# Two conditioned sequence layers: key exponentials of layer 0 scaled on POOL and turned by DVE blocks and a scratch in batches 1 to 6

## The reference, cut to what matters

```python
xn = _ln(x, ln_w, ln_b)
q = xn @ Wq + bq
k = xn @ Wk + bk + (1.0 - src_mask) * -1000000.0
q = softmax(q.reshape(b, t, h, dh), axis=-1)
k = softmax(k.reshape(b, t, h, dh), axis=1)          # over the tokens
v = ((xn @ Wv + bv) * src_mask).reshape(b, t, h, dh)
att = einsum('bnhd,bnhl->bhdl', k, v)
y = einsum('bnhd,bhdl->bnhl', q, att).reshape(b, t, d)
hh = _ln(y, ln2_w, ln2_b) * (1.0 + scale) + shift    # scale, shift from silu(emb) @ W_emb
return x + silu(hh) @ W_out + b_out
```

## Time and profile before

| | |
|---|---|
| median of three runs | 1324.58 us (1324.13 to 1326.19) |
| profiled execution | 1324.74 us |
| its span, first to last instruction | 1322.9 us |
| mean granted TensorE clock | 0.969 |
| PE busy | 1265.4 us, 96% |
| PE's weight loads busy | 1010.9 us, 76% |
| DVE busy | 1012.7 us, 77% |
| ACT busy | 902.6 us, 68% |
| POOL busy | 499.3 us, 38% |
| layer 0 | to about 470 us, layer 1 behind it |

### The profile page before, as it was taken

How to read it: one execution, slowest core, us unless ns; L and a number is a source line. 1 busy time by engine, 2 the same in 40 slices (tenths; PEclk the granted TensorE clock), 3 DMA queues, 4 the chain that set the end, 5 groups by cost and what they waited for, 6 DMA issues and landing times.

```text
span 1322.9 us, 24811 instructions
## 1 busy us (share of the span) xinstructions
PE 1265.4 (96%) x9256; PEld 1010.9 (76%) x9256; DVE 1012.7 (77%) x2027; ACT 902.6 (68%) x2051; POOL 499.3 (38%) x451
## 2 busy tenths in 40 slices
PE   8998999999999799899999999999999999999998
PEld 6786888888888687577787788788788788788666
DVE  6678898898988856766876876876876876877766
ACT  5232433424326438788898898898898898898984
POOL 0526548366383730102612612612612512522502
PEclk9998999999999899899999999999999899999989
DMA  9245374664646455855455465464465464454422
GB/s 334 76 152 156 101 222 121 206 194 120 214 127 215 144 197 174 241 164 162 149 172 158 152 174 156 152 175 149 158 174 150 150 182 144 153 172 144 136 75 81
DMA packets 123081, 214.13 MB, mean 162 GB/s; under 512 B 8704, under 2 KB 38456, under 8 KB 122064
## 3 DMA queue, kind: packets, MB, share of 16 engines
q1 hardware_dynamic: 122960, 212.55, 52.1%
HBM read 130.14 MB, written 81.85 MB: 160 GB/s over the span
## 4 chain that ended last, share of the span: by engine, by line
PE 64%; DVE 13%; ACT 11%; POOL 7%; issue 4%; DMA 1%; SPq 0%; DVEq 0%; POOLq 0%; ACTq 0%
PE ps L612 13%; PE ps L613 12%; PE ps L614 12%; PE ps L794 8%; PE ps L768 6%; PE ps L776 6%; ACT ps L958 5%; PE ps L607 3%; DVE st L1080 2%; ACT Pb L968 2%; PE ps L719 2%; POOL yb L1388 2%; DVE xr L1098 2%; POOL yb L1444 1%; POOL vt L1395 1%
## 5 line engine op out<-in xcount | busy, mean ns | idle before, releaser
L958 ACT ACTIVATE ps<-ps,cT 128x512 f32<-128x512 f32 x512 | 346.8, 717 | 19.6 <-DVE cT L1243 19.2
L1243 DVE TENSOR_REDUCE cT<-ps 128x1 f32<-128x512 f32 x512 | 320.6, 682 | 43.8 <-PE ps L768 42.2
L968 ACT ACTIVATE Pb<-ps 128x512 f32<-128x512 f32 x512 | 268.5, 661 | 46.0 <-PE ps L776 43.8
L768 PE MATMUL ps<-Ks,Qs 98*128 98x512 f32 x512 | 185.0, 423 | 16.7 <-ACT ps L958 16.5
L776 PE MATMUL ps<-Qs,Ks 100*128 100x512 f32 x512 | 159.1, 408 | 1.1 <-ACT ps L958 0.5
L768 PEld LDWEIGHTS ps<-Ks,Qs 98*128 98x128 f32 x512 | 96.6, 192 | 67.2 <-ACT ps L958 41.8
L958 ACT ACTIVATION_READ_ACCUMULATOR ps<-ps,cT 128x1 f32 x512 | 134.8, 263 | 0.0
L776 PEld LDWEIGHTS ps<-Qs,Ks 100*128 100x128 f32 x512 | 95.8, 189 | 37.8 <-ACT Pb L968 12.8
L612 PE MATMUL ps<-xTh,Wh_k 128*128 128x512 f32 x256 | 105.6, 413 | 14.0 <-DVE xTl L1102 11.0
L612 PE MATMUL ps<-Wh_o,sTh 128*128 128x512 f32 x256 | 104.7, 409 | 5.1 <-DVE sTl L1220 4.5
L1379 POOL TENSOR_SCALAR vf<-vf,mk 128x512 f32<-128x512 f32 x16 | 25.0, 1564 | 209.7 <-DVE vf L1153 209.7
(11 more groups left out here) (178 smaller groups left out, 2826.3 us busy)
## 6 DMA issues: line engine op xcount, KB each, us to landing
Qs<-stack_scratch SPq DMA_DIRECT2D x32, 768.0 KB
Ks<-stack_scratch SPq DMA_DIRECT2D x32, 768.0 KB
stack_scratch<-sg_q SPq DMA_DIRECT2D x32, 512.0 KB, 2.7
stack_scratch<-sg_k SPq DMA_DIRECT2D x32, 512.0 KB, 2.6
wr<-in_x SPq DMA_DIRECT2D x32, 256.0 KB, 5.0
x_scratch<-wr SPq DMA_DIRECT2D x32, 256.0 KB, 2.4
stack_scratch<-sg_q SPq DMA_DIRECT2D x32, 256.0 KB, 2.9
stack_scratch<-sg_k SPq DMA_DIRECT2D x32, 256.0 KB, 3.0
```

The source lines that it names most:

```text
L768: e.matmul(bank[:], Qs[par][0:RX, j, t * 128:(t + 1) * 128], Ks[par][0:RX, j, :], start=True, stop=True).then_inc(s["S"], 1)
L958: e.activation(bank[:], bank[:], ACT.Exp, bias=nx[:, n % 2, j, t, 0:1], accum_out=dn[:, b % 2, t, 4 * g + j:4 * g + j + 1]).then_inc(s["S_ ...
L968: e.activation(Pb[m][:, j, :], ps[bank_of["a", n, m, j]][:], ACT.Exp).then_inc(s["P"], 1)
L1243: e.tensor_reduce(nx[:, n % 2, j, t, 0:1], ps[bank_of["S", n, j, t]][:], AX.X, ALU.max, negate=True).then_inc(s["S_max"], 1)
```

## The change

Only layer 0 changes.

1. POOL multiplies ET by krc (`en`, four operations of 128x512 a batch, in all eight batches), behind all four exponentials. The reciprocal of the sums moves to its own part, and A0 becomes a plain copy.
2. In batches 1 to 6 (`e_by_scratch`) PE's transposes and ACT's copies of ET are gone. DVE transposes the 32x32 blocks of ET in place (`ex`), and SP writes ET to `e_scratch` in four DMAs and reads Et back in one (`eio`). The state matmuls wait for that DMA. Batches 0 and 7 keep the turn on PE, behind POOL's scaling.
3. In those six batches ACT writes the exponentials in blocks (`E_tile`), and the host regroups Wk's columns and bk (`turn_k`), so that the blocks come back in the order of the channels; ACT's copies in batches 0 and 7 put them in order.
4. In `tx`, the subtraction xTl of a tile stands behind the L1098 of the next tile, and not behind its own.
5. The next batch's mask is made behind `ex` in batches 1 to 6.
6. `PLAN` has new numbers for layer 0 ("0x", "f", "1t", "1v") and for the weights of layer 1 ("we"); `LAG` has three new entries. Four semaphores are merged into others.

The numbers of the table, the order and the layout of ET:

```diff
-    "0x": ((0.548, 0.792), (0.83, 0.879), (0.518, 1.2), (0.573, 0.91), (0.427, 0.744), (0.345, 0.783), (1.195, 1.2), (0.846, 0.866), (0.777, 0.79), (0.424, 0.754), (1.161, 1.2), (0.149, 0.872), (0, 0.398), (0.735, 1.136)),
+    "0x": ((0.544, 0.678), (0.828, 0.84), (0.902, 0.924), (0.508, 0.742), (0.431, 0.916), (0.623, 0.839), (1.2, 1.2), (0.793, 0.909), (0.788, 0.8), (0.571, 0.814), (1.07, 1.178), (0.124, 0.949), (0.066, 0.422), (0.688, 0.741), (0.079, 0.563), (0.635, 0.637), (0.226, 0.987)),
...
-        L0.append((tiles("te", b), *lag(1)))
+        L0.append((tiles("en", b), *lag(14)))
+        if e_by_scratch(b):
+            L0.append((tiles("ex", b), *lag(15)))
+            L0.append(([("eio", b)], *lag(16)))
+        else:
+            L0.append((tiles("te", b), *lag(1)))
...
+def e_by_scratch(b):
+
+    return 0 < b < 7
...
+        def E_tile(b, g):
+
+            if e_by_scratch(b):
+                return ET[:].rearrange("p g n -> p (g n)").rearrange("p (c g i) -> p c g i", g=NC, i=32)[:, :, g, :]
+            return ET[:, g, :].rearrange("p (c i) -> p c i", i=32)
```

PE, the state matmuls:

```diff
-                    e.wait_ge(s["E_t"], 4 * b + 4)
+                    e.wait_ge(*((s["e_in"], 16 * b) if e_by_scratch(b) else (s["E_t"], e_turned(b, 3))))
```

ACT, before batch b's first exponential:

```diff
-                        e.wait_ge(s["E_tr"], 4 * b)
+                        e.wait_ge(*((s["e_out"], 64 * (b - 1)) if b > 1 else (s["E_tr"], 4)))
```

DVE, the subtraction:

```diff
-                if i == 1 and turned_on_host(x):
-                    e.wait_ge(s["xT_hi"], 4 * x + c + 1)
-                    e.tensor_tensor(xTl[:, c, :], xr[:, c, :], xTh[:, c, :].bitcast(F32), ALU.subtract).then_inc(s["xT_lo"], 1)
+                if turned_on_host(x):
+                    for u in ((c - 1,) if i == 0 and c else (3,) if i == 1 and c == 3 else ()):
+                        e.wait_ge(s["xT_hi"], 4 * x + u + 1)
+                        e.tensor_tensor(xTl[:, u, :], xr[:, u, :], xTh[:, u, :].bitcast(F32), ALU.subtract).then_inc(s["xT_lo"], 1)
```

DVE, new parts:

```diff
+            def en(i, b, t):
+                if t == 0:
+                    e.wait_ge(s["k_exp"], 4 * b + 4)
+                    e.reciprocal(krc[:, b % 2, :], ksm[:, b % 2, :]).then_inc(s["k_rc"], 1)
+
+            def ex(i, b, g):
+                e.wait_ge(s["e_n"], 4 * b + g + 1)
+                e.transpose(E_tile(b, g), E_tile(b, g)).then_inc(s["e_bt"], 1)
+                if g == 3:
+                    mask(b + 1)
```

DVE, A0's copy:

```diff
-                    e.tensor_tensor(A0[r, :, r], part, krc[r, b % 2, :].unsqueeze(2).to_broadcast([64, NC, 64]),
-                                    ALU.mult).then_inc(s["A_c"], 1)
+                    e.tensor_copy(A0[r, :, r], part).then_inc(s["A_c"], 1)
```

POOL, a new part:

```diff
+            def en(i, b, g):
+                e.wait_ge(s["k_rc"], b + 1)
+                e.tensor_scalar(E_tile(b, g), E_tile(b, g), krc[:, b % 2, g:g + 1], None, ALU.mult).then_inc(s["e_n"], 1)
```

SP, a new part:

```diff
+            def eio(i, b):
+                if i == 0:
+                    e.wait_ge(s["e_bt"], 4 * b)
+                    if b > 1:
+                        e.wait_ge(s["e_in"], 16 * (b - 1))
+                    blocked = ET[:].rearrange("p g n -> p (g n)").rearrange("p (c n) -> p c n", n=128)
+                    for a in range(4):
+                        e.dma_start(eTd.rearrange("(c r) d -> r c d", r=32)[:, :, 128 * a:128 * a + 128],
+                                    blocked[32 * a:32 * a + 32]).then_inc(s["e_out"], 16)
+                else:
+                    e.wait_ge(s["e_out"], 64 * b)
+                    e.wait_ge(s["att"], b)
+                    e.dma_start(Et[:], eTd.rearrange("(t p) d -> p t d", p=128)).then_inc(s["e_in"], 16)
```

Host:

```diff
+    turn_k = np.arange(D).reshape(4, NC, 32).transpose(1, 0, 2).reshape(D)
```

More of the change, by code:

```diff
@@ L865, in k @@
                     if g == 0 and b:
-                        e.wait_ge(s["E_tr"], 4 * b)
+                        e.wait_ge(*((s["e_out"], 64 * (b - 1)) if b > 1 else (s["E_tr"], 4)))
                     e.wait_ge(s["k_nb"], 4 * b + g + 1)
-                    e.activation(ET[:, g, :], vt[g % 2][:], ACT.Exp, bias=knb[:, p, g:g + 1],
+                    e.activation(E_tile(b, g), vt[g % 2][:].rearrange("p (c i) -> p c i", i=32), ACT.Exp, bias=knb[:, p, g:g + 1],
                                  accum_out=ksm[:, p, g:g + 1]).then_inc(s["k_exp"], 1)
@@ L874, in te @@
                         e.wait_ge(s["att"], b)
-                    e.wait_ge(s["E_tr"], 4 * b + t + 1)
-                    e.copy(Et[:, t, :], ps[bank_of["te", b, t]][:]).then_inc(s["E_t"], 1)
+                    e.wait_ge(s["E_tr"], e_turned(b, t))
+                    e.copy(Et[:, t, :].rearrange("p (a g i) -> p g a i", a=4, g=NC),
+                           ps[bank_of["te", b, t]][:].rearrange("p (g a i) -> p g a i", a=4, g=NC)).then_inc(s["E_t"], 1)
             def v(i, x, t):
@@ L981, in prologue @@
                 e.memset(A0[:], 0.0).then_inc(s["a_set"], 1)
-                e.memset(lnc[:], 0.0).then_inc(s["ln_set"], 1)
+                e.memset(lnc[:], 0.0).then_inc(s["a_set"], 1)
                 e.memset(nxs[:].bitcast(F32), 0.0).then_inc(s["nx_set"], 1)
@@ L1145, in v @@
                         e.wait_ge(s["l_bv"], 32)
-                    if x < 8 and t == 0:
-                        e.wait_ge(s["k_exp"], 4 * x + 4)
-                        e.reciprocal(krc[:, x % 2, :], ksm[:, x % 2, :]).then_inc(s["k_rc"], 1)
                     e.wait_ge(s["v_mm"], n)
@@ L1188, in sta @@
                 e.wait_ge(s["att"], b + 1)
-                e.wait_ge(s["k_rc"], b + 1)
                 if b:
@@ L1676, in _ @@
             prologue()
-            parts = {"w": w, "m": m, "nx": nx_, "tx": tx, "k": k, "qio": qio, "yio": yio, "ty": ty, "o": o, "ahead": ahead, "stacks": stacks, "narrow": narrow, "qk": qk,
+            parts = {"w": w, "m": m, "nx": nx_, "tx": tx, "k": k, "eio": eio, "qio": qio, "yio": yio, "ty": ty, "o": o, "ahead": ahead, "stacks": stacks, "narrow": narrow, "qk": qk,
                      "stack": stack, "nxt": nxt, "lx": lx, "lr": lr, "end": end}
@@ L1705 @@
         "cT": np.ascontiguousarray(g["cond_2048"].T.reshape(8, 128, B).transpose(1, 0, 2)),
-        "cols0": np.concatenate([col(g[P0 + n]) for n in ("ln_w", "ln_b", "ln2_w", "ln2_b", "bq", "bk", "b_emb")], axis=1),
+        "cols0": np.concatenate([col(g[P0 + n][turn_k] if n == "bk" else g[P0 + n]) for n in ("ln_w", "ln_b", "ln2_w", "ln2_b", "bq", "bk", "b_emb")], axis=1),
         "cols1": np.concatenate([col(g[P1 + n]) for n in ("norm_w", "norm_b", "sb_norm_w", "sb_norm_b", "q_b", "k_b", "emb_b")], axis=1),
         "xT0": np.ascontiguousarray(g["x"].transpose(0, 2, 1).reshape(B, NC, 128, T).transpose(0, 2, 1, 3)),
-        "Wq0": g[P0 + "Wq"], "bq0": g[P0 + "bq"], "Wk0": g[P0 + "Wk"],
+        "Wq0": g[P0 + "Wq"], "bq0": g[P0 + "bq"], "Wk0": g[P0 + "Wk"][:, turn_k],
         "Wv0": g[P0 + "Wv"], "bv0": g[P0 + "bv"], "We0": g[P0 + "W_emb"],
```

50 lines of the change are left out of this document (25 added, 25 removed), and 4 rows, old and new, of the table PLAN.

## The result

The changed kernel takes 1346.44 us (1344.83 to 1349.73, four runs) against 1324.36 us for the kernel before on the same chip: 1.0171 of it, 95% interval 1.0152 to 1.0189. It is 22.1 us slower. The forecast was 1334, inside a range of 1312 to 1347. The profiled execution took 1346.03 us, its span is 1344.2 us. The granted TensorE clock fell from 0.969 to 0.958.

The account below looks back on a forecast made before the run. PE was taken to bound leg A, and DVE, POOL and ACT Leg B. Per batch +0.6 (Leg B) and +0.9 (leg A), over six batches +9.0 us on 1324.74: 1333.7 us, range 1312 to 1347, the forecast's own 1328 to 1340.

Parts of the forecast that it names:

- Leg B: Layer 0 batch, q tile 1 done to k product's last xTl: 24.38 us, set by DVE, POOL, ACT; forecast +0.6 us.
- a better and a worse case: Leg B's last subtractions: -0.6 us if POOL stays out of the way, +1.0 with an eq multiplication ahead of both.
- leg B's end is set by POOL's row: POOL's row to the last xr keeps its operations, ending 20.9 us into Leg B; only what follows on DVE changes.
- leg A: Rest of the batch, from k's last xTl to q tile 1: 29.14 us, set by PE; forecast +0.9 us.
- contention with the three scalings: In leg A, three POOL scalings of ET beside DVE's L1209, L1214, L1220: 1.2 us, bounds nothing to 3.0.
- The mask operation: In leg A, DVE's mask on mB beside POOL's xr: up to 0.91 us instead of 0.42, 0.5 more taken.
- the time joins PE's wait: In Leg B, the removed transposes' 1.76 us a batch only lengthens PE's wait for xTl: no gain counted.
- the start: New positions in batch 0 (and the change to layer 1): costed at nothing, 3 us either way for the range.
- The transfers: ET's scratch trip, about 15 us, against state matmuls about 18 us after q tile 1: 3 us cover, cost nothing.
- PE sets the pace: Rival, faster: Leg B gets shorter by 1.8 us, so the transposes' 1.76 us a batch is gained; 1314 us, chance 0.30.
- The clock falls: Rival: longer PE wait before k slows the clock, 1.6 us in leg A hiding DVE's 0.9; 1338 us, chance 0.10.
- POOL doesn't give way: Rival, slower still: scalings cost 3.0 us, 2.7 net in leg A, 1.0 in Leg B; 1347 us, chance 0.08.

Follow-up runs that it names:

- e1: Kernel before with one PE transpose of ET instead of four per tile in batches 1 to 6: 1328.59 us, 1.0033 of the kernel before.
- e3: Changed kernel without POOL's four multiplications of ET, A0's copy multiplying by krc again: 1333.81 us, 1.0074 of the kernel before.
- e5: Changed kernel with the subtraction L1124 back behind the L1119 of its own tile: 1336.84 us, 1.0101 of the kernel before.
- e6: Changed kernel with two POOL additions (L1440) behind the last xr scale and two DVE L1256 behind the last xTl: 1337.30 us, 1.0102 of the kernel before.
- e9: Changed kernel with the multiplication of xr by the layer norm's weights (L1119, four a batch) moved from DVE to ACT: 1311.82 us, 0.9901 of the kernel before.
- e10: e9 with ET scaled on ACT instead of POOL and L1124 back behind its own tile: 1304.75 us, 0.9840 of the kernel before.
- e8: Changed kernel with PE kept busy by zero-tile products in its waits for xTl, batches 2 to 7: 1336.56 us, 1.0100 of the kernel before.
- e12: e10 with the modulation of y (L1237, four a batch in layer 0) on ACT too: 1302.17 us, 0.9825 of the kernel before.
- e11: Kernel before with the multiplication L1098 moved from DVE to ACT: 1318.68 us, 0.9941 of the kernel before.

## Why the prediction was wrong, point by point

**Right: what bounds the kernel.** Leg B belonged to DVE, POOL and ACT, and twelve of the sixteen transposes, 1.25 us a batch, gave nothing when they were taken out alone (e1). They went into PE's waits. In the changed kernel these waits are 1.03 + 3.38 us a batch instead of 0.57, with the growth of leg B in them.

**Wrong: leg B +0.6 us; it was +2.6.** Two parts. The last two subtractions: I laid out a better and a worse case and took a value between; the worse one, +1.0, is what e3 and e5 measure (+0.96). In the batch that won the layout comes true row by row: the two qdn end 21.9 us into the leg, xf3 at 22.4 and xTl3 at 25.30, where the sum had 21.9, 22.4 and 25.35. The other part is not in the prediction at all: the first L1119, far from the end of the leg, cost 1.6 us in the batches that lost. The step that failed is the sentence that leg B's end is set by POOL's row, ended at 20.9 us, with only the tail changing. POOL's row was in time: its last xr ended 20.3 us into the leg where the race was lost and 20.8 where it was won, and when e6 brought it forward to 17.8 the leg was still 24.2 us. DVE's row was late: it came to the two qdn at 21.4 us where the race was lost, at 20.2 where it was won. It has a chain of its own from the first xr on, as its operations meet POOL's.

**Wrong: leg A +0.9 us; it was +2.2.** The contention with the three scalings was sized at 1.2 us; the rows of DVE give 1.2 (L1237 0.92, L1242 1.06, two L1248 1.78 against 0.54, 0.69 and 1.29 when alone), e3 gives 1.0 for DVE's row and e9 against e10 gives 0.7 for the leg. The mask operation took 0.38 us: the 0.5 us for contention there was nothing. Without the clock leg A is 29.88 us (e8), +0.7, so this part of the sum was near. What failed is the term left out of it, the clock. I gave it 1.6 us, but only in a rival with a chance of 0.10, although my own sum had PE's waits grow to "2 to 4 us a batch", and the row that shows what such waits do stood in the prediction. e8 measures 1.48 us, e5 1.3 to 1.6. That row was even read too mildly: the last waits ahead of its slow stretch, in the kernel before, are not the one of 4.3 us, behind which it was back at 1.00 by 117.5 us, but two of about 1 us.

```profile
118.50 0.51 PE L612 MATMUL ps<-xTh,Wh_k 128*128 128x512 f32 x1 [1.15 <-DVE xTl L1102]
120.42 0.50 PE L612 MATMUL ps<-xTh,Wh_k 128*128 128x512 f32 x1 [0.94 <-DVE xTl L1102]
```

So the step "the time joins PE's wait", costed at nothing, had a price.

**The sum, laid out again.** For a batch that lost the race: order of the subtractions 0.96, race 1.60, clock 1.48, scalings 0.68, together 4.72 us, against 58.24 - 53.53 = 4.71. So exact a fit proves nothing, as the terms of a leg are steps between the same end points (leg B 24.32, 25.28, 26.88; leg A 29.20, 29.88, 31.36). What bears them out is that the points between come back in other kernels: 24.32 in e5's won batches; 29.88 in e8, e9 and the one leg A of e5 at full clock; 29.20 in e10. The terms aren't independent either: in a batch that wins the race the slow clock takes back part of the gain (leg A 31.93), and the waits of 2.8 us that are left without order and race still bring it (e5).

**Also at nothing in the sum: the start.** The new positions in batch 0 were costed at nothing, with 3 us either way. The changed kernel is 5.5 us behind at q tile 1 of batch 2, a quarter of the loss. No run takes this apart; e9, with four operations moved to ACT, is ahead of the kernel before at that point (148.92 us). The six equal batches of the forecast were in truth two of start, four with +4.3 us on the mean, and a period into batch 7 that had no spare time on DVE before the change either.

**Right: the transfers.** The middle batches cost nothing, as the 3 us of cover said.

**The rule on the port.** I set the lock of the Trainium skill (SBUF — State Buffer, "SBUF: two separate sides") against batch 7's rows, in which POOL mostly gave way. The runs are on the side of the lock where POOL's operation has two tensor inputs: a waiting DVE operation took 3.11 us, while three of POOL's (L1423, L1440, L1399) ran at their full speed. The Trainium skill says there that whoever starts first keeps the port for the whole instruction; who goes next it leaves open, and here the waiting operation was passed over twice, by L1440 and by L1399.

**The rivals.** "PE sets the pace" was given 0.30 and doesn't happen in this kernel (e1); the prediction had put its point of decision at 22.6 us for leg B, and e10 and e12, with 22.6, stand just at it. "The clock falls" did come true as a mechanism, but not with DVE's 0.9 us hidden in it. "POOL doesn't give way", 1347 us, came nearest in time, and that is mostly luck: its 1.0 us in leg B is there, its 3.0 us for the scalings is not (0.7 to 1.2), and race and clock fill the gap.

## What to carry to other kernels

Time taken off an engine that waits anyway becomes more waiting, and on TensorE waiting has a price of its own: count the clock's loss (here 1.3 to 1.6 us a batch) into every sum that makes PE's waits longer. Where DVE and POOL both work on SBUF without a pause, count operations first (four fewer took leg B from 25.28 us, with the race won, to 22.6), their order second (0.96 us); here the way to shorten such a stretch was to give some of them to ACT, and then a change that failed could pay (1.0171 became 0.9840). The Trainium skill says as much (Perfetto Trace Analysis, "Optimizing Scalar/DVE Operations"): work of a saturated DVE may go to the Scalar engine, and shifting it between DVE and GpSimd may not help, as they share a port. The runs agree with the first half (e9, 1.0171 to 0.9901; e11, 0.9941); no run here shifted work between DVE and GpSimd.
